# Stack of six graph layers on one core: orders of the engines, the loads at the beginning, and the join of layer 0's heads

## What is computed

```python
# layer 0: 8 heads of 32 features, biases
q, k, v = x @ Wq + bq, x @ Wk + bk, x @ Wv + bv
attn = softmax(where(adj == 0, -inf, q @ k.T * 32**-0.5))     # per head
x = layernorm((attn @ v) @ Wo + bo + x) * gamma + beta
# layer 1: one head of 256 features
sc = where(adj == 0, -inf, (x @ Wq) @ (x @ Wk).T * 256**-0.5)
x = layernorm(x + (softmax(sc) @ (x @ Wv)) @ Wo + bo) * gamma + beta
# layers 2 to 5: q and k of 128 features
attn = softmax(where(adj == 0, -1e10, (x @ Wq.T + bq) @ (x @ Wk.T + bk).T / 128**0.5))
x = layernorm(x + (attn @ x) @ Wc.T) * ln_g + ln_b
```

## Time and profile before

| | |
|---|---|
| median of 3 runs | 2533.27 us (2532.14 to 2534.21) |
| the profiled execution | 2531.23 us, its span 2529.4 us |
| busy of the span | PE 2382.8 (94%), PEld (weight loads) 2182.5 (86%), DVE 1553.4 (61%), ACT 1570.5 (62%), POOL 1841.4 (73%) |
| granted TensorE clock, mean | 0.99 |
| DMA | 68.62 MB, mean 27 GB/s; 206 GB/s over the first 40 us |

### The profile page before, as it was taken

How to read it: one execution, slowest core, us unless ns; L and a number is a source line. 1 busy time by engine, 2 the same in 40 slices (tenths; PEclk the granted TensorE clock), 3 DMA queues, 4 the chain that set the end, 5 groups by cost and what they waited for, 6 DMA issues and landing times.

```text
span 2529.4 us, 57112 instructions
## 1 busy us (share of the span) xinstructions
PE 2382.8 (94%) x20944; PEld 2182.5 (86%) x20944; DVE 1553.4 (61%) x4874; ACT 1570.5 (62%) x5512; POOL 1841.4 (73%) x2439
## 2 busy tenths in 40 slices
PE   5899999999999999999999999999999999999985
PEld 4789889889889889889889889889888888888874
DVE  2566666666666666666666666666666666666663
ACT  4666666666666666666666666666656656656642
POOL 3577777777777777777777777777777777777773
PEclk8999999999999999999999999999999999999997
DMA  3000000000000000000000000000000000000000
GB/s 141 22 26 22 24 31 22 25 30 20 27 31 18 28 31 18 28 31 18 29 30 18 28 30 18 28 30 18 28 31 18 29 31 18 28 31 12 14 10 13
DMA packets 38150, 68.62 MB, mean 27 GB/s; under 512 B 4336, under 2 KB 12656, under 8 KB 37232
## 3 DMA queue, kind: packets, MB, share of 16 engines
q1 hardware_dynamic: 37872, 64.97, 7.5%
HBM read 48.18 MB, written 16.78 MB: 26 GB/s over the span
## 4 chain that ended last, share of the span: by engine, by line
PE 58%; DVE 13%; ACT 12%; POOL 12%; issue 3%; DMA 0%; DVEq 0%; SPq 0%; POOLq 0%
PE qk_bank L374 12%; PE value_bank L382 11%; ACT probs L607 8%; PE unit_bank L374 7%; PE context_bank L527 6%; PE unit_bank L437 4%; POOL rstd L909 4%; PE qk_bank L480 4%; PE unit_bank L382 4%; DVE xT_lo L771 4%; POOL x_out L928 3%; POOL x_out L930 3%; PE unit_bank L449 3%; DVE y L825 2%; DVE y L806 2%
## 5 line engine op out<-in xcount | busy, mean ns | idle before, releaser
L928 POOL TENSOR_TENSOR x<-y,rows 128x512 f32<-128x512 f32 x320 | 407.9, 1275 | 280.2 <-DVE y L825 280.2
L825 DVE TENSOR_SCALAR y<-y,mv,rstd 128x256 f32<-128x256 f32 x768 | 280.7, 408 | 362.1 <-POOL rstd L909 362.0
L627 ACT CAST xT_hi<-qk_bank 128x512 fp32r<-128x512 f32 x320 | 191.2, 598 | 449.7 <-PE qk_bank L480 449.7
L374 PE MATMUL qk_bank<-xT_hi,w_lo 128*128 128x256 f32 x1280 | 405.4, 317 | 67.0 <-DVE xT_lo L771 67.0
L930 POOL TENSOR_TENSOR x<-x,rows 128x512 f32<-128x512 f32 x320 | 412.5, 1289 | 25.1
L607 ACT ACTIVATE probs<-unit_bank,negmax 128x128 f32<-128x128 f32 x1024 | 366.0, 384 | 49.9 <-DVE negmax L743 49.9
L382 PE MATMUL value_bank<-w_lo,xT_hi 128*128 128x256 f32 x1280 | 393.1, 307 | 0.0
L806 DVE SCALAR_TENSOR_TENSOR y<-context_bank,rtotal,x 128x256 f32<-128x256 f32 x640 | 277.2, 474 | 155.6 <-PE context_bank L527 155.6
L374 PE MATMUL qk_bank<-xT_lo,w_hi 128*128 128x256 f32 x1280 | 361.7, 283 | 0.0
L382 PE MATMUL value_bank<-w_hi,xT_lo 128*128 128x256 f32 x1280 | 361.6, 283 | 0.0
L374 PE MATMUL qk_bank<-xT_hi,w_hi 128*128 128x256 f32 x1280 | 360.5, 282 | 0.0
(11 more groups left out here) (89 smaller groups left out, 6339.1 us busy)
## 6 DMA issues: line engine op xcount, KB each, us to landing
x0T<-xT_in SPq DMA_DIRECT2D x64, 256.0 KB, 2.6
x<-x_in SPq DMA_DIRECT2D x64, 256.0 KB, 2.6
out<-x_out SPq DMA_DIRECT2D x64, 256.0 KB, 2.1
adj<-adj_in SPq DMA_DIRECT2D x64, 128.0 KB, 2.2
rows<-rows_in SPq DMA_DIRECT2D x1, 1920.0 KB, 11.4
probs0T<-w_in SPq DMA_DIRECT2D x1, 1024.0 KB, 5.1
probs<-w_in SPq DMA_DIRECT2D x1, 1024.0 KB, 8.1
x<-w_in SPq DMA_DIRECT2D x1, 1024.0 KB, 14.0
```

Source lines behind the costliest of these rows:

```text
L374: mm = pe.matmul(psum[:, n * G * N:(n + 1) * G * N], split(w, name, kd, at, at + P), flat(xT_half[:, kd]), start=kd == 0 and w is w_lo, st ...
L825: m = dve.tensor_scalar(y[:, r, g], y[:, r, g], mv[:, r, g, 0:1], rstd[:, r, g:g + 1], ALU.subtract, ALU.mult)
L928: pool.tensor_tensor(new, y[:, r], row_of_each(f"gamma{layer}"), ALU.mult).then_inc(zg_ready, 1)
```

## The change

- **The join.** `wo0` becomes one of the split weights. ACT casts the heads to `headsT_hi`, DVE subtracts for `headsT_lo` right behind its `split_lo` of that slot, and `join_heads` makes 12 float32r products instead of 4 float32 ones.
- **POOL.** `scale_and_shift` is cut in two. An item's `shift` now stands behind the group's `find_rstd`. `normalise_probs0` of unit 1 comes behind the item's `find_rstd`.
- **ACT and DVE.** The exps of unit 1 move from the end of one slot to the next, those of unit 2 to its end; `move_v` of the late values comes behind the exps. DVE's reciprocal of unit 1 moves back with them.
- **The beginning.** x comes first, the first chunk in four pieces with a semaphore each, each split for itself, and the rows of constants in two. PE waits at each product for its own weights. `fuse_layer1` moves one slot back, and its split two. Chunk 1 is staged in `late_weights`, where chunk 3 is loaded once the fusing is done. Chunks 2 and 3 are split in four pieces, by ACT and DVE instead of ACT and POOL, in slots 1, 5, 9 and 13.

```diff
+FIRST_WEIGHTS = ["wv0", "wq0", "wk0", "wo0"]
+LATER_SLOTS = [STEP * (layer - 1) for layer in range(2, LAYERS)]
+LATER_LEAD = 3
...
             def join_heads(group):
-                pe.wait_ge(headsT_ready, group + 1)
-                for g in range(G):
-                    for kd in range(KD):
-                        mm = pe.matmul(join_bank[:, g * D:(g + 1) * D], headsT[:, kd, g], wo0[:, kd],
-                                       start=kd == 0, stop=kd == KD - 1)
+                pe.wait_ge(headsT_lo_ready, group + 1)
+                if group == 0:
+                    pe.wait_ge(w0_lo_ready, FIRST_WEIGHTS.index("wo0") + 1)
+                for g in range(G):
+                    mm = values(join_bank, headsT_hi, headsT_lo, "wo0", g)
                 mm.then_inc(join_in_psum, 1)
...
-            pe.wait_ge(w0_lo_ready, 1)
-            pe.wait_ge(eye16_ready, 1)
             for i in SLOTS:
...
-                if i == -7:
+                if i == -6:
                     fuse_layer1()
...
             def move_headsT(group):
                 act.wait_ge(headsT_in_psum, group + 1)
-                act.copy(flat3(headsT[:, :]), heads_bank[:, :]).then_inc(headsT_ready, 1)
+                if group > 0:
+                    act.wait_ge(join_in_psum, group)
+                act.copy(flat3(headsT_hi[:, :]), heads_bank[:, :]).then_inc(headsT_hi_ready, 1)
...
+                if i == FIRST:
+                    for name in FIRST_WEIGHTS:
+                        split_first(name)
                 if item(i - 1):
                     softmax(i - 1)
-                if item(i - 1) and late_values(i - 1):
-                    move_v(i - 1)
                 if (group := due(i, 6)) is not None:
                     exp0(group, 0)
                 if (group := due(i, 5)) is not None:
-                    exp0(group, 2)
+                    exp0(group, 1)
...
+                if item(i - 1) and late_values(i - 1):
+                    move_v(i - 1)
                 if item(i):
                     move_qk(i)
                 if item(i - 1):
                     move_probsT(i - 1)
-                if (group := due(i, 6)) is not None:
-                    exp0(group, 1)
+                if (group := due(i, 5)) is not None:
+                    exp0(group, 2)
...
+            def split_headsT(group):
+                dve.wait_ge(headsT_hi_ready, group + 1)
+                dve.tensor_tensor(flat3(headsT_lo[:, :]), heads_bank[:, :], flat3(headsT_hi[:, :]).bitcast(F32),
+                                  ALU.subtract).then_inc(headsT_lo_ready, 1)
...
+                if i + LATER_LEAD in LATER_SLOTS:
+                    n = LATER_SLOTS.index(i + LATER_LEAD)
+                    dve.wait_ge(later_hi_ready, n + 1)
+                    split_weight(later_at[n], LATER, later_staged(n)).then_inc(later_lo_ready, 1)
...
                 if (group := due(i, 5)) is not None:
                     normalise_probs0(group, 0)
-                    normalise_probs0(group, 1)
...
                 if item(i - 2):
                     find_rstd(("item", i - 2))
+                if (group := due(i, 5)) is not None:
+                    normalise_probs0(group, 1)
                 if item(i - 1):
                     keep_valid(i - 1)
                 if item(i - 2):
-                    scale_and_shift(("item", i - 2))
+                    scale(("item", i - 2))
+
                 if (group := due(i, 2)) is not None:
                     find_rstd(("group", group))
-                    scale_and_shift(("group", group))
...
+                if item(i - 2):
+                    shift(("item", i - 2))
+                if (group := due(i, 2)) is not None:
+                    scale(("group", group))
+                    shift(("group", group))
```

142 lines of the change are left out of this document (83 added, 59 removed).

## The result

The changed kernel takes 2491.01 us (median, 2490.31 to 2491.72) where the kernel before took 2532.93 in runs beside it (2532.14 to 2534.21): a ratio of 0.9834, 95% interval 0.9817 to 0.9851, or 42 us saved. The forecast was 2437 with a range of 2405 to 2478, so the direction was right and the size wrong: 54 us are missing of the 97 expected.

What follows compares the result with a forecast made beforehand. PE was taken as the bound, losing 2.03 of 38.06 us per period to waits. Gains of 20.5 (join), 63.8 (full periods), 12.4 (beginning) and 0 (later weights), 96.7 us, took 2533.3 to 2436.6; range 2405 to 2478.

Steps and rivals of the forecast that it cites:

- A: PE's wait for xT_lo before the projection in the slot behind the join: 0.74 us lost per period.
- B: PE's transpose of the next x, idle for ACT's kT: 0.50 us lost per period, expected to stay at 0.53.
- C: PE's wait for xT_lo one slot after A, behind unit 1's exps on ACT: 0.79 us lost per period.
- The floor: PE's period between joins if packed without waits: some 36.0 us.
- The join: Layer 0's heads on PE: 12 single products take 0.32 us less per group, 20.5 us over 64 groups.
- POOL's order (A): The group's rstd ahead of the item's shift makes xT_lo earlier at A: 0.70 us gained per period.
- The exponentials (B and C): Moving unit 1's exps from ahead of xT_hi on ACT: C gains 0.71 us per period, B loses 0.03.
- D: ACT's v copy, now behind the exps, frees PE's value bank late: 0.28 us lost per period, bounds 0 and 1.55.
- The beginning, 12.4: Start of the kernel: first matmul near 6.4, first join at 32.6 instead of 45.15; 12.4 us gained, between 9 and 15.
- The later weights, 0: Four split pieces on ACT and DVE: 2 us cost, 2 given back for thin-period waits; exclusion with POOL at most 5.
- Weight loads show: Rival, chance 0.03: twelve weight loads make the join 2.3 us instead of 1.74, giving 2490 us.
- The exps only change places: Rival, chance 0.17: D or a late negmax takes back most of C, 0.4 to 0.7 us per period, 2460 to 2478.

Runs made afterwards that it cites:

- run 13: run 1 plus v copied before the exps, group's x shifted before x_out, x_out's shift put off a period, unit 0's exps split around q and k: 2407.9 us.
- run 14: run 13 with the join of before (fp32 products) in place of the three products of halves: 2425.7 us.
- run 4: The kernel before with only the join changed to three products of high and low halves: 2533.6 us against 2533.4.
- run 9: run 1 with v copied ahead of layer 0's exps, and the join of before put back: 2428.0 us, the same as with the new join.
- run 1: The changed kernel with POOL's scale of the group moved ahead of the item's shift, so no pass stands beside DVE's y pair: 2451.1 us.
- run 5: The kernel before with only the order of layer 0's exps changed, with v's copy, reciprocal and unit 1's normalising moved along: 2503.0 us.
- run 3: The kernel before with only POOL's item shift moved behind the group's rstd: 2530.1 us against 2533.4.

## Why the prediction was wrong

Point by point, in its order.

- **What bounds the kernel**: right. A, B and C were the losses, and runs 13 and 14 have a steady period without waits. The floor was too low by 0.45, though: 36.0 was worked out with the old join, and run 14, which has it, takes 36.47. Of this 0.13 is A, from the context product to the piece behind the projection: it takes 2.40 in every run without a wait there, where I took 2.27 from another place of the period.
- **The join, 20.5 us**: the duration was right (1.42), the sentence "PE is packed around the join, so 0.32 to 0.33 comes off" was wrong. Packed around it is not packed behind it: some 6 us behind it PE waits at A for a chain that does not pass through the join, and the earlier trace rows had that chain's later half. The saving fell into A (run 4: 0 us), as long as any wait hung on that chain (run 9: 0 us), and appeared in full when none did (run 14: 17.8 us).
- **POOL's order (A), 0.70 a period**: `rstd` came where I put it (5.17 for 5.14). The step that failed is "The DVE rows behind it come at the same distances": y's 0.73 became 1.67 since the shift I moved was put beside it, and `xT_lo` starts 7.14 behind the join's start instead of 6.17 (7.19 before). I costed the moved pass by who needs its result, and never by who runs beside it. Run 1 gives 0.93 of it back; A and the join together brought 0.06 us a period of 1.02 forecast, some 56 us in all, which is the whole of the miss. Putting A right alone doesn't reach the forecast: run 1 is at 2451, 14 us above it, since B and D then cost more.
- **The exponentials (B and C)**: right. C gained 0.74 (forecast 0.71), B nothing (forecast -0.03). Alone 30 us (run 5).
- **D**: right in kind, place and about in size: 0.22 for 0.28. In run 1 it rose to 0.44, since PE came earlier: the price of one wait depends on the others.
- **The beginning, 12.4**: PE's pieces of the chain, to set beside the earlier trace rows:

```profile
6.60 2.90 PE unit_bank L406 x12
...
30.54 1.48 PE unit_bank L406 x12
...
41.50 2.90 PE qk_bank L398 x12
```

  The first product is at 6.60 (forecast 6.4) and the first join at 30.54 for 45.15, 14.6 gained. The first projection of the later layers, 55.91 before and 41.50 now, shows 14.4 of it. Then some 3.4 are lost in the thin periods. PE's rows of the changed kernel there name part:

```profile
58.67 0.39 PE L406 MATMUL unit_bank<-w_lo,headsT_hi 128*128 128x256 f32 x1 [1.14 <-DVE headsT_lo L785]
...
84.78 0.90 PE L469 MATMUL unit_bank<-eye,probs 128*128 128x128 f32 x4 [3.79 <-POOL probs L966]
```

  The first hangs on the subtraction that I had costed at nothing (0.6 of the 1.14), which costs nothing only in a full period. The second was 3.25 before. Over the two stretches of 50 us behind the beginning (36 to 136; 50 to 150 before) the granted clock was 0.89 and 0.94, before 0.92 and 0.98, which is 3.5 us of full clock. The pieces of the later weights stand in the same stretch, as the next point shows; how the 3.4 divide was not tested. About 11 us stay, within the 9 to 15.

  From the last join to the end it takes 114.5 us, 2.2 more than before. The wait for `xT_lo` right behind that join is 3.0 where it was 2.1, and behind it the granted clock fell, for a part of the 6 us from 2381 to the lower level of 1.2 GHz: 0.72 over these, where the kernel before had 1.00 at the same distance from its last join. Run 1, with y short, waits 2.1 there, has 1.00, and needs 112.0. The length of that wait alone doesn't decide on the clock: run 3 also waits 2.1 and takes 114.1.
- **The later weights, 0** (2 for the pieces, 2 given back): no run leaves them out, but the trace has them on the chain. The first two pieces stand there with ACT's casts (0.96 at 52.19, 0.94 at 74.12) and DVE's subtractions behind these (1.20 and 1.03, "issue" in the chain), 4.1 us in all, between the first projection and the third join; and 3.2 of the 3.4 us are lost there. The trace also shows the exclusion that I priced at 5 us at most. DVE, then POOL, in the changed kernel:

```profile
53.16 1.31 DVE L759 TENSOR_TENSOR w_lo<-x,w_hi 128x1024 fp32r<-128x1024 f32 x1 [1.03 <-ACT w_hi L702]
```

```profile
53.36 2.26 POOL L947 TENSOR_TENSOR x<-x,rows 128x512 f32<-128x512 f32 x1
...
132.20 2.19 POOL L979 TENSOR_TENSOR x<-y,rows 128x512 f32<-128x512 f32 x1 [0.85 <-DVE y L868]
```

  Two of the four pieces (at 53.16 and 132.03) had a POOL pass beside them, which took 2.26 and 2.19 us where they take 1.30 and 1.28 otherwise, some 1.9 us on POOL. And at the beginning the subtraction for `wv0`, two SBUF inputs too, took 1.26 us (from 5.20) beside POOL's `x0T_lo`, which had started at 4.64, where the next one of its size takes 0.68; the first product waits for it. "No row of before has the two side by side" was a misreading. `w_lo` of the first chunk ran from 7.76 for 1.76 us, and POOL beside it:

```profile
9.01 1.63 POOL L889 TENSOR_TENSOR x0T_lo<-x0T,x0T_hi 128x512 fp32r<-128x512 f32 x1 [8.20 <-ACT x0T_hi L586]
```

  The other `x0T_lo` take 1.29. That row should have sent me to look at who stands beside whom wherever a pass moves. I held the rule of the Trainium skill ("SBUF — State Buffer", "SBUF: two separate sides") only against these subtractions, for their two SBUF inputs. y has one SBUF input beside its scalars; whether it runs in the 2-port mode that the same sentence names, no trace shows.
- **The sum**: 11 + 58 x 0.54 = 42, less 2 at the end, against 41 in span (2529.4 to 2488.5).
- **The range**: by its own terms (3 for the beginning, 0.4 a period) the forecast's part ends at 2463 and not at 2458; it changes nothing here.
- **The rivals**: none was this. "Weight loads show" (2490) came nearest in time, by luck: the join takes 1.42 and not 2.3. "The exps only change places" (2460 to 2478) is refuted by run 5. I wrote that a period above 37.2 should send the reader to `value_bank` and layer 0's transposes; the place was `xT_lo`.

Still open: why y beside a pass ends only 0.15 behind it, which of y's properties makes it wait, and how the 3.4 us behind the beginning divide.

## What to carry to other kernels

Before adding a saving on the bound engine to the sum, walk back from the *next* wait behind it: if that wait's chain left the engine ahead of the saved work, the saving is worth nothing until that wait is gone. And when a pass of one engine is moved, look not only at who needs its result but at what stands beside it in its new place, instruction by instruction; GpSimd beside an fp32 SBUF-to-SBUF `tensor_scalar` of VectorE is a place to avoid. When the order is mended, test the parts again: the join was worth 0 us twice and 18 the third time.

## What the runs showed of the hardware

A VectorE `tensor_scalar` of 128x256 in fp32, from SBUF to SBUF with two scalars per partition, takes 407 ns alone, 697 beside GpSimd instructions of 0.6 us, 811 each when two of them meet two halves of a pass, and 1348 beside one of 1.27 us; a stride of two leaves it so (1350). In each of the held kinds it ends 0.15 us behind the GpSimd instruction, and the spread within a kind is at most 12 ns, so chance has little part in it. VectorE's `scalar_tensor_tensor` with a PSUM operand (474 ns on average before, 477 after) showed nothing of it.

A VectorE `tensor_tensor` with two SBUF inputs and a GpSimd `tensor_tensor` of 128x512 held each other in whichever order they came: VectorE's took 1255 ns for 677 where GpSimd had started 0.56 us earlier, and ended 0.55 behind it; GpSimd's took 2262 and 2186 for some 1290 where VectorE had started 0.2 earlier, and ended 1.13 to 1.14 behind it.
